# Four constant bf16 matmuls on TensorE ahead of two waits in every batch of a graph-attention kernel

## The reference

```
xn = layernorm(x)
h  = (xn @ W)                       # 8 heads of 32 channels
e  = leaky_relu(a1[src] + a2[dst])  # one number per edge and head
ex = exp(e - max over the target's edges)
out[dst] = sum over its edges of h[src] * ex / sum over its edges of ex
x = x + out + mix(xn)               # mix: q/k/v products, a 256x256 kv matrix, an output product
x = x + moe_ffn(layernorm(x))       # two chosen experts, gelu, layer norm
```

## Time and profile before

| | us |
|---|---|
| median of 3 runs | 3226.48 |
| lowest, highest | 3215.01, 3229.0 |
| the profiled execution | 3193.87 |
| its span | 3192.1 |
| first pass, edge stage, last stage (from the span's start) | 0 to 120, to 2737, to 3192 |
| granted share of TensorE's clock over the span | 0.788 |

### The profile page before, as it was taken

The page is one execution under the profiler, slowest core; times in us unless marked ns, Lnnn a source line. Parts: engine busy times, 40 slices in busy tenths (PEclk is TensorE's granted clock), DMA queues, the critical chain, the costliest instruction groups (busy, mean ns, idle before and its releaser), DMA issues.

```text
span 3192.1 us, 36971 instructions
## 1 busy us (share of the span) xinstructions
PE 2246.7 (70%) x8328; PEld 1471.7 (46%) x8329; DVE 1733.2 (54%) x3616; ACT 885.9 (28%) x1862; POOL 1676.3 (53%) x1821
## 2 busy tenths in 40 slices
PE   6566767676676666766667666777777765479997
PEld 4444444444444444444434434445444443157776
DVE  6455555555555555555555556565656555824334
ACT  3422222222222222222222223222222222334332
POOL 3566666666666666666666666666666666000000
PEclk9777777777777777777777777787877777689999
DMA  7444444444444444444444444444444444110000
GB/s 239 132 119 117 114 113 123 115 122 115 115 116 121 113 123 114 114 119 119 120 114 115 115 120 124 128 134 127 134 127 133 129 117 114 15 31 15 20 20 21
DMA packets 174887, 346.37 MB, mean 109 GB/s; under 512 B 38430, under 2 KB 91268, under 8 KB 174852
## 3 DMA queue, kind: packets, MB, share of 16 engines
q0 software_dynamic: 83296, 234.42, 27.0%
q1 hardware_dynamic: 91268, 111.28, 11.9%
q10 hardware_dynamic: 288, 0.26, 0.0%
HBM read 319.49 MB, written 26.33 MB: 108 GB/s over the span
## 4 chain that ended last, share of the span: by engine, by line
PE 39%; another core or an unknown queue 20%; issue 17%; DVE 15%; DVEq 4%; ACT 3%; DMA 1%; SPq 0%; POOL 0%; ACTq 0%
PE bank L920 15%; PE bank L1033 5%; DVE acc L1338 5%; PE bank L1023 4%; PE bank L929 3%; DVE zs L1308 3%; DVEq L1322 3%; PE bank L938 2%; PE bank L927 2%; PE bank L972 2%; PE bank L974 1%; PE bank L885 1%; PE bank L832 1%; ACT work L698 1%
## 5 line engine op out<-in xcount | busy, mean ns | idle before, releaser
L613 POOL DMA_INDIRECT work<-h_tab,idx x1712 | 1624.4, 949 | 983.8 <-issue 459.3
L920 PE MATMUL bank<-work 128*128 128x264 f32 x3424 | 1210.1, 503 | 722.7 <-DVE acc L1338 548.5
L920 PEld LDWEIGHTS bank<-work 128*128 128x128 f32 x3424 | 769.0, 243 | 1046.3 <-DVE acc L1338 647.0
L1338 DVE TENSOR_TENSOR acc<-bank,acc 128x264 f32 x854 | 366.5, 429 | 878.9 <-remote 579.6
L1330 DVE TENSOR_TENSOR work<-work,bank 128x1024 f32<-128x1024 f32 x428 | 520.3, 1216 | 170.5 <-issue 165.5
L706 ACT ACTIVATE bank<-zb 128x64 f32<-128x64 f32 x214 | 48.7, 228 | 1824.2 <-DVE zb L1313 1333.3
L1223 DVE TENSOR_TENSOR work<-bank,cols 128x1024 f32<-128x1024 f32 x215 | 260.9, 1214 | 0.0
L700 ACT ACTIVATE work<-work,ones 128x1024 bf16<-128x1024 bf16 x215 | 246.8, 1148 | 7.0
L698 ACT ACTIVATE work<-work,pcol 128x1024 bf16<-128x1024 bf16 x215 | 243.4, 1132 | 12.0 <-DMA work<-dst_d 12.0
L640 POOL COPY work<-acc 128x768 f32 (+2 forms) x17 | 13.6, 805 | 374.0 <-PE bank L985 296.3
L1023 PE MATMUL bank<-work 128*128 128x384 f32 (+1 forms) x544 | 177.6, 481 | 13.8 <-DMA work<-L_ffn_b 7.6
(11 more groups left out here) (244 smaller groups left out, 1920.1 us busy)
## 6 DMA issues: line engine op xcount, KB each, us to landing
work<-dst_d SPq DMA_DIRECT2D x216, 256.0 KB
work<-h_tab,idx POOLq DMA_INDIRECT x1712
xnt_c<-xnt_d SPq DMA_DIRECT2D x66, 128.0 KB
h_tab<-acc SPq DMA_DIRECT2D x49, 132.0 KB
xnt_d<-acc SPq DMA_DIRECT2D x49, 128.0 KB
q2t_d<-q2t_c SPq DMA_DIRECT2D x49, 128.0 KB
out<-wqkv SPq DMA_DIRECT2D x16, 384.0 KB, 2.5
X<-x SPq DMA_DIRECT2D x5, 1024.0 KB, 10.0
```

The costliest lines, as they stand in the source:

```text
L613: nc.gpsimd.indirect_dma_start(out=ring[q][:, j, :], out_offset=None, in_=h_tab, in_offset=bass.IndirectOffsetOnAxis(ap=idx[:, q, j:j + 1] ...
L920: ins = mm(bank[MB[(q * SB + s) % len(MB)]][:, 0:TW], hot[q][:, s * G + g, :], ring[q][:, s * G + g, :], start=(g == 0), stop=(g == G - 1))
L1338: v.tensor_tensor(a, bank[MB[(q * SB + s) % len(MB)]][:, 0:TW], a, ALU.add).then_inc(added, 1)
```

## The change

A constant FILL = 4 is added. In TensorE's `batch` the wait for `added` goes to the head of each step, and at steps 0 and 2 it is followed by four bf16 matmuls of a constant 128x128 block with 512 constant columns (both from `a2p`, the table that the picks read), written to the bank that the step's own sums then overwrite (`start=True`). Only after them come the waits for `msg_ready` and `den_ready`.

```
-                for s in range(SB):
-                    if s % HS == 0:
-                        pe.wait_ge(msg_ready, b * 2 + s // HS + 1)
...
+                for s in range(SB):
+                    wait(pe, added, b * SB + s + 1 - len(MB))
                     if s % HS == 0:
+                        for _ in range(FILL):
+                            mm(bank[MB[(q * SB + s) % len(MB)]][:], a2p[:, 0:P], a2p[:, 0:512], start=True, stop=True)
                         pe.wait_ge(msg_ready, b * 2 + s // HS + 1)
                     if s == 0:
                         pe.wait_ge(den_ready, b + 1)
-                    wait(pe, added, b * SB + s + 1 - len(MB))
                     for g in range(G):
                         ins = mm(bank[MB[(q * SB + s) % len(MB)]][:, 0:TW], hot[q][:, s * G + g, :], ring[q][:, s * G + g, :],
                                  start=(g == 0), stop=(g == G - 1))
```

More of the change, by code:

```diff
@@ L43 @@
 HS = SB // 2
+FILL = 4
 MB = [3, 4]
```

## The result

| | before | after |
|---|---|---|
| median of the timed runs, us | 3224.47 (3215.01 to 3229.0) | 3249.05 (3247.9 to 3253.61) |
| ratio after / before | | 1.0087, 95% interval 1.0068 to 1.0106 |
| profiled execution, us | 3193.87, span 3192.1 | 3248.15, span 3246.3 |
| granted TensorE clock over the span | 0.788 | 0.878 |

The account below looks back on a forecast made before the run. A ring of waits in the edge stage, above GpSimd's gathers, bounds the kernel. Per batch 2.5 us added less 1.35 saved, times 0.17, over 214 batches gives 40 us: 3226.5 + 40 = 3266 us, range 3150 to 3400.

Parts of the forecast that it names:

- absorbed in the main: Edge stage: VectorE's wait hides most of the added TensorE time; +40 us, 3266 us, chance 0.50.
- case "slower": Whole kernel: slower by more than the about 0.5% that a measurement can tell; chance 0.53 over all cases.
- case "nothing": Edge stage: all of the added matmul time is absorbed; 3226 us, chance 0.15.
- The ring and its floor: Edge stage: VectorE, TensorE and GpSimd wait for each other; beneath, eight gathers take 10.0 of 12.2 us a batch.
- The extreme of the clock rival: Edge stage: at full clock unnamed releases come early too and gathers bound; 470 us saved, 2756 us, chance 0.04.
- The order of the waits: TensorE, steps 0 and 2: `added` was the last wait to end before too, so moving it costs nothing.
- the groups behind the last wait: TensorE, steps 0 and 2: new matmuls fill no wait, standing behind the last one and ahead of the sums.
- The price of a group: Four new matmuls at step 0 or 2: 1.0 us at full clock, 2.0 us at half; 428 groups.
- The clock: TensorE, edge stage: clock rises half of the way from 0.75 to full, saving 1.35 us a batch.
- What reaches the time: Edge stage batch: of net 1.15 us more on TensorE, 0.17 reaches the time; 0.19 us a batch, 40 us.
- the release is tied to the gathers in flight and not to TensorE's end: VectorE's step 0 add: starts 2.3 us after GpSimd's last gather began, so the wait absorbs TensorE's time.
- In line: Step 0's group is paid in full every batch: 214 us at full clock, 3440 us, up to 428 us; chance 0.15.

Follow-up runs that it names:

- the change again: The changed kernel, no edit, timed again beside the kernel before: 2726.53 us, ratio 1.0005.
- the imitated release: Both kernels edited: GpSimd waits for its last gathers, then copies 512 columns to let VectorE's step 0 add go: 3454.31 us before, 3460.6 us with the change.

## Why the prediction was right, and where it was not

*The forecast.* The likeliest case, absorbed in the main and slower by 40 us, came as 25 us (54 between the profiled executions, against which the sum was made). Its interval, 0.68% to 1.06%, lies above the 0.5% that the prediction gave as noise, so in the first measurement this is its case "slower". In the later measurements, without late releases, the case "nothing" holds: 1.0005.

*The ring and its floor.* Right in kind. The prediction put GpSimd's eight gathers, 10.0 us, beneath the 12.2 us of a batch, and without the unnamed waits a batch is those 10.0 us. The kernels with whole gathers share one sum: span less the idle time before the gathers is 3192.1 - 983.8 = 2208 us before, 2207 after, 2200 for the change again, 2202 with the group at step 0 alone, 2197 with eight there, and 3452.4 - 676.4 - (120.8 + 452.4) = 2203 us with the imitated release, whose copy counts there too:

```profile
L619 POOL DMA_INDIRECT work<-h_tab,idx x1712 | 1623.4, 948 | 676.4 <-issue 455.4
...
L609 POOL CAST pad<-cols 128x512 f32 (+1 forms) x198 | 120.8, 610 | 452.4 <-DMA work<-h_tab,idx 452.4
```

This is bookkeeping and no proof of who sets the pace. It says that the gathers' own time and all that lies before the first and behind the last of them stay the same, so that every microsecond of difference stands as idle time before some gather. VectorE's work is constant too (busy 1733, 1733 and 1737 us in the first three), and it would pass the same test. That GpSimd is the bound in the later measurements rests on two other things: it never waits there beyond its own 0.3 us, and with half the gathers the kernel takes 9% less. In the first measurement it was not the bound: it waited 325.0 us for unnamed releasers. The extreme of the clock rival, 2756 us, was the time of a kernel without the unnamed waits; it is 2724 us, and no edit is needed for it.

*The order of the waits, and the groups behind the last wait.* Right: 1.0002 for the first; 606.9 us of waits before line 918 and 36.6 before line 923 for the second.

*The price of a group.* 1.0 us at full clock and 2.0 us at half were taken; the timeline has 1.03 us with its tail and 0.87 us until the next matmul, 1.89 and 1.68 us at half clock.

The Trainium skill (TensorE: Matmul & The Clock Gate, Back-to-back issue gap) gives 0.86 and 1.7 us; the trace agrees with it.

*The clock.* Half of the way from 0.75 to full was assumed, 0.875; 0.87 came, although TensorE is as idle before step 2 as it was (606.9 us of waits, 548.5 before). That half was a guess between two arguments, not worked out from rows.

The Trainium skill (the same page, HAM oscillation), as the prediction read it, would have left the clock where it was, since the new matmuls stand behind the stretch. The measurement decides: 0.87.

*What reaches the time.* The forecast was 1.15 us more on TensorE and a share of 0.17 of it, 0.19 us a batch. The traces have 12.47 - 12.20 = 0.27 us, the medians 25 / 214 = 0.12 us. The size fits, in part by luck, because two terms err in opposite directions. TensorE's busy time grew by 92.7 us over the whole kernel (2246.7 to 2339.4), 0.43 us a batch and not 1.15: the groups are busy for 2.3 us a batch, where 2.5 were taken, but the higher clock gave back 1.9 where 1.35 were taken. (139 of the 1712 new matmuls have no record in the trace; with some 0.2 us for each it would be 0.6 us at most.) Of these 0.43 to 0.6 us between 0.2 and 0.6 reached the time, not 0.17. The reason given for the share does not fully hold either. The step that failed is "the release is tied to the gathers in flight and not to TensorE's end": VectorE's unnamed waits did not get shorter with their ends fixed, they grew from 579.6 to 629.1 us (with those before X, from 588.2 to 757.0), and the end moved from 2.40 to 2.91 us after the last gather. The 2.3 us that the prediction read in two batches was not a fixed distance before the change, as the quarters above show. With a release that really is tied to the gathers, the imitated one, the change costs 6 to 12 us. That the rest, up to the 25 us, came by the release itself being later is argued from this and from the pair of traces, not shown. Why it was later stays open, since no later run showed late releases, and so does whether the new matmuls did it.

*In line.* This rival (a group paid in full at step 0) did not hold for the change, but it is real one step away: the half change with its group at step 0 alone is 2.8% slower and eight there 6.5%, because there the step 0 groups of the q = 0 batches run cold. Even so they are not paid in full: 76 us over 214 batches are 0.36 us of a group that takes 1.25 us on average until the sums. I had priced the two groups alike, and their roles differ: step 0's stands on the path, step 2's in slack, and the second pays for the first. That was measured where the gathers set the pace; in the first measurement the two groups were not separated.

## What to carry to other kernels

A filler on one engine can only matter by what it adds to or takes from the waits of the engine that sets the pace. Which engine that is does not come out of a sum of busy and idle time, which balances for every engine with constant work. It comes out of an engine that never waits (here GpSimd, at most 0.3 us before a gather) and of a run in which its work is cut (half the gathers, 9% less). A filler that raises the granted clock (0.75 to 0.87) earned nothing where TensorE is not what that engine waits for; with TensorE nearer to the bound it earned 0.5 us a batch in one stage and cost 0.6 us in the other, so it has to be measured. Where it stands matters: four matmuls in slack at step 2 cost nothing, the same four at step 0, at the head of the work on the path, cost 76 us, and both together cost nothing again. No filler here made the kernel with its full work faster.

## What the runs showed of the hardware

The same kernel took 3224 us in the first measurement and 2724 us in three later ones on two chips. The traces differ in two things. In the first, semaphore events of TensorE come late. Counted from the end that the trace models for the matmul, those of the last matmul of a step (`summed`) come a median of 0.46 us after it, a quarter of them more than 2.56 us; those of the picks 2.20 us at the median; in the changed kernel 1.41 and 3.98 us. Events of several matmuls come in one burst: in the kernel before, those of a qk product, of the picks and of steps 0 and 1, with modelled ends from 1506.43 to 1508.50 us, all stand between 1512.15 and 1512.37. In the later traces all are 0.01 us. In the first they are late only while gathers run: in the kernel before, half of TensorE's recorded events between the first gather (50.9 us) and the last (2716.6 us) are over 0.1 us late, none of the 42 ahead of them. No recorded event of another engine is late in that stretch.

The second difference is that many events are not recorded at all in the first measurement: of the 7685 semaphore updates that the five engines' instructions make, the trace of before holds 5592 and that of the changed kernel 5488, on every engine; the later traces hold all but a few. A wait without a name may be a late event or a missing one, and the waits of the first measurement have to be read with that in mind. The waits themselves are real: with them goes the extra 460 us of idle time before the gathers (983.8 against 523.5).

What brings it on is open; it was not reproduced, only imitated. The chip of the first measurement is not on record, so a property of that chip is not excluded, nor is the recording of the profile itself. A cause found in one measurement, such as this ring with its pause, should be looked for in a second one before a kernel is tuned to it.
